# A half tile's inner rows are turned before the next unit's gate and up products, and its down product comes one unit after it instead of two

## The reference, cut to what matters

```python
logits = x @ gate_w.T                        # 64 experts, TOP_K = 8 of them per token
topv, topi = jax.lax.top_k(logits, TOP_K)
gu = jnp.einsum('nh,eih->nei', x, gu_w)      # gate and up rows, 2 x 128 inner
gate, up = (gu[..., :I], gu[..., I:])
inter = jax.nn.silu(gate) * up
inter_w = inter * W[:, :, None]              # routing weight, zero where not chosen
out = jnp.einsum('nei,ehi->nh', inter_w, dp_w)
```

## Time and profile before

| | |
|---|---|
| median of 3 runs | 970.89 us (968.95 to 973.75) |
| span of the profiled execution | 965.6 us |
| PE matmul busy | 872.5 us, 90% of the span |
| DVE, POOL, ACT busy | 465.5, 458.7, 214.3 us |
| mean of what DMA moved | 229 GB/s over the span |

### The profile page before, as it was taken

How to read it: one execution, slowest core, us unless ns; L and a number is a source line. 1 busy time by engine, 2 the same in 40 slices (tenths; PEclk the granted TensorE clock), 3 DMA queues, 4 the chain that set the end, 5 groups by cost and what they waited for, 6 DMA issues and landing times.

```text
span 965.6 us, 12358 instructions
## 1 busy us (share of the span) xinstructions
PE 872.5 (90%) x3437; PEld 514.2 (53%) x3437; DVE 465.5 (48%) x1177; ACT 214.3 (22%) x559; POOL 458.7 (48%) x447
## 2 busy tenths in 40 slices
PE   6999989989988694979989998999999999986997
PEld 2434534534534343657666665666666666763442
DVE  4797785788586540423323323333233333324496
ACT  2022221321312111212232222322223222321000
POOL 1420055236355766357556666566665656655000
PEclk9999999999998697989999999999999999998999
DMA  9951003103003152788898998889998997899997
GB/s 341 326 163 71 1 8 96 45 2 104 1 1 115 41 190 73 229 289 277 289 322 272 339 323 315 307 286 338 325 319 302 311 333 262 283 354 402 382 419 315
DMA packets 76927, 221.36 MB, mean 229 GB/s; under 512 B 19078, under 2 KB 19462, under 8 KB 76472
## 3 DMA queue, kind: packets, MB, share of 16 engines
q1 hardware_dynamic: 48760, 149.12, 43.9%
q0 software_dynamic: 28096, 71.42, 21.0%
HBM read 183.98 MB, written 48.87 MB: 241 GB/s over the span
## 4 chain that ended last, share of the span: by engine, by line
PE 60%; issue 8%; DVE 7%; another core or an unknown queue 7%; DMA 4%; SPq 3%; ACT 2%; ACTq 0%; POOL 0%; DVEq 0%; POOLq 0%
PE bank L2026 17%; PE bank L2046 8%; PE bank L1798 7%; PE bank L2016 5%; PE bank L1845 5%; PE bank L1911 3%; PE bank L2136 3%; DMA front<-y_rows 3%; PE bank L2037 2%; PE bank L1809 2%; SPq L668 2%; PE bank L2054 1%; PE bank L1930 1%; DMA front<-h_rows,gid_fixed 1%
## 5 line engine op out<-in xcount | busy, mean ns | idle before, releaser
L2026 PE MATMUL bank<-h2T,wqkv 128*128 128x256 f32 x1024 | 243.1, 388 | 9.9 <-issue 9.6
L719 POOL DMA_INDIRECT slot_table<-pair,place x128 | 130.4, 1019 | 183.3 <-DVE place L1262 118.2
L2026 PEld LDWEIGHTS bank<-h2T,wqkv 128*128 128x128 f32 x1024 | 193.1, 194 | 41.1 <-issue 16.5
L775 POOL DMA_INDIRECT y_rows<-front,tbl x110 | 113.6, 1033 | 83.8 <-DVE front L1641 38.1
L766 POOL DMA_INDIRECT front<-h_rows,gid_fixed x112 | 115.8, 1034 | 69.1 <-issue 31.6
L2046 PE MATMUL bank<-wqkv,front 128*128 128x512 f32 x256 | 127.9, 621 | 11.2 <-DVE front L1622 7.5
L1641 DVE TENSOR_SCALAR front<-bank,wgt 128x512 f32<-128x512 f32 x146 | 107.1, 748 | 43.3 <-DMA y_rows<-front,tbl 19.8
L1006 ACT ACTIVATE h2T<-bank 128x512 f32<-128x512 f32 x148 | 82.2, 595 | 161.4 <-issue 65.6
L1798 PE MATMUL bank<-wqkv,front 128*128 128x512 f32 x256 | 113.5, 594 | 0.0
L1622 DVE TENSOR_TENSOR front<-bank,front 128x256 f32<-128x256 f32 x64 | 27.2, 424 | 177.4 <-ACT front L1016 135.2
L2016 PEld LDWEIGHTS bank<-const,front 128*128 128x128 f32 x592 | 69.1, 143 | 62.0 <-issue 47.4
(11 more groups left out here) (292 smaller groups left out, 860.1 us busy)
## 6 DMA issues: line engine op xcount, KB each, us to landing
wqkv<-in_experts SPq DMA_DIRECT2D x64, 768.0 KB
front<-in_experts SPq DMA_DIRECT2D x36, 512.0 KB
front<-y_rows SPq DMA_DIRECT2D x20, 768.0 KB, 12.4
front<-in_experts SPq DMA_DIRECT2D x36, 256.0 KB
wqkv<-y_rows SPq DMA_DIRECT2D x12, 768.0 KB, 13.4
front<-in_w_mod SPq DMA_DIRECT2D x5, 1024.0 KB, 10.1
x<-in_x SPq DMA_DIRECT2D x4, 1024.0 KB, 10.8
h_rows<-h SPq DMA_DIRECT2D x4, 1024.0 KB
```

The costliest lines, as they stand in the source:

```text
L719: pool.indirect_dma_start(out=slots[:, :], out_offset=bass.IndirectOffsetOnAxis(ap=place[b % 2][:, i, k:k + 1], axis=0), in_=pair[:, b * T ...
L775: pool.indirect_dma_start(out=y_rows[:, :], out_offset=bass.IndirectOffsetOnAxis(ap=to, axis=0), in_=yb[s], in_offset=None, bounds_check=P ...
L2026: mm = pe.matmul(pair_bank[u % 2][:, j * PAIR:(j + 1) * PAIR], w[:, at:at + INNER], xT[u % 2][:, k, :], start=(k == 0), stop=(k == KC - 1))
```

## The change

On PE the turning of a half unit's inner rows moves from behind the gate and up products of the next unit to ahead of them, right behind the next tokens' transpositions. Its down product moves from two units behind to one unit behind, so that each unit now has exactly one unit's down products. DVE's scaling of the half tile and SP's wait for its down product move with it. After a half unit R the order on PE becomes: products of R, down of R-1, turn tokens of R+2, **turn inner rows of R**, products of R+1, **down of R**, turn tokens of R+3, products of R+2, down of R+1.

```diff
@@ -635,10 +635,8 @@
             for u in range(BODY_UNITS + 1):
                 if u in REST_UNIT:
                     next_rest_gu(u)
-                if u - 2 in REST_UNIT:
-                    after_down(UNIT[u - 2][0])
-                if u > 3 and u - 1 not in REST_UNIT:
-                    after_down(UNIT[u - 1][1])
+                if u > 3:
+                    after_down(UNIT[u - 1][-1])
@@ -1645,8 +1643,8 @@
             def taken(u, r):
-                for b in [u - 2] * (u - 2 in REST_UNIT) + [u - 1] * (u >= 1 and u - 1 not in REST_UNIT):
-                    for n in UNIT[b]:
+                if u:
+                    for n in UNIT[u - 1]:
                         take_y(n, r)
@@ -2084,15 +2082,16 @@
             def downs(u, r):
-                if u - 2 in REST_UNIT:
-                    n = REST_UNIT.index(u - 2)
-                    pe.wait_ge(s_rest_down, 32 * (n + 1))
-                    down_rest(u - 2)
-                if u >= 1 and u - 1 not in REST_UNIT:
+                if u - 1 in REST_UNIT:
+                    pe.wait_ge(s_rest_down, 32 * (REST_UNIT.index(u - 1) + 1))
+                    down_rest(u - 1)
+                elif u:
                     down(u - 1, r, slot_of(u - 1))
 
             def body(u):
                 turn(u + 1, 0)
+                if u - 1 in REST_UNIT:
+                    turn_inter(u - 1)
                 if u == 0:
                     pe.wait_ge(s_sht, TPB * (HELD + 1))
                 if u == 1:
@@ -2105,8 +2104,6 @@
                     gate_up(u, 0, slot_of(u))
-                if u - 1 in REST_UNIT:
-                    turn_inter(u - 1)
                 downs(u, 0)
```

## The result

| | before | after |
|---|---|---|
| median of the timed executions of this comparison | 968.83 us (964.38 to 975.74, 20 runs) | 977.53 us (969.81 to 984.79, 20 runs) |
| time and span of the profiled execution | span 965.6 us | 979.93 us, span 978.1 us |

The ratio is 1.0081, 95% interval 1.0057 to 1.0105: the change makes the kernel slower by 0.8%. Every timed execution of the changed kernel carries a span and a clock of its own (1.8 to 1.9 us between its time and its span, median clock 0.960 over the twenty), so the timed executions do what the profiled one does; that undoes the choice on which the forecast stood.

What follows compares the result with a forecast made beforehand. PE was taken as the bound, lacking 15.3 of 376 us. Minus 1.3 (bank wait), minus 0.9 (seams) and 0 for the rest gave a span of 963.4, with 5.3 us above the span 968.7 us; range 957 to 1003.

Steps and rivals of the forecast that it cites:

- The down product: Half tile's down product on PE, one unit earlier: bank wait gone, minus 1.3 us; cheaper seams between matmul groups, minus 0.9.
- the faster rival: Late marks are real, but the new order covers them where they cost PE: minus 13 us, 958 us; chance 0.17.
- The transposition: Turning of inner rows on PE: its new wait for silu and product, 0.65 us, has 2.70 us of cover, costs 0.
- The disputed term: Whether PE's marks, up to 5.9 us late to ACT in the profile, are late in timed executions; the forecast chose no.
- DVE: 0: DVE's copy of turned rows is never late and one scaling moves a unit earlier: 0 in either direction.
- SP and POOL: 0: SP's wait and loads and the half tile's scatter come earlier: taken as 0, ends minus 2 and plus 2 us.
- slower, by the new wait: PE stalls at the turning for late marks, 8 times 3.9 and 8 times 0.7 us: plus 20, 991 us; chance 0.28.
- Slower, with the clock: Each 3.9 us stall also halves PE's clock for 3.3 us, 13 us more: 1004 to 1018 us; chance 0.05.
- The sum and the range: Minus 2.2 us on the 965.6 us span, plus 5.3 us: 968.7 us, no change; range 957 to 1003 us.
- The marks come once PE stands still: PE's standstill at the turning releases late marks, stalls of 1.3 us in 8 to 16 units: 964 to 975 us; chance 0.10.

Runs made afterwards that it cites:

- e12: Changed kernel without POOL's gathers of the body's tiles from 16 on, scatters kept; one execution, span 935.8 us, 0.969 of the kernel before.
- e14: Changed kernel with the gathers of the body's tiles from 16 on cut to 16 of 128 rows; one execution, 1.004 of the kernel before.
- e2: Kernel before with only the half unit's down product moved to one unit behind, right behind the unmoved turning; 955.51 us against 958.69, ratio 0.9957.
- e1: Kernel before with only the turning of inner rows moved ahead of the next unit's products; 998.5 us against 958.69, ratio 1.0407.
- e13: Kernel of e10 with the half unit's down product moved behind the next tokens' transpositions; 963.88 us against 967.99 for the kernel before, ratio 0.9931.
- e10: Changed kernel with the turning of inner rows amid the next pair unit's up products; 952.9 us against 959.68 for the kernel before, ratio 0.9922.
- e3: Changed kernel with the turning of inner rows between the next unit's gate and up products; 949.72 us against 958.69 for the kernel before, ratio 0.9912.
- e4: Changed kernel with half units' gate and up products over the whole array, not two column halves; one execution, 1.008 of the kernel before.
- e7: Changed kernel with the gathers of the body's tiles from 16 on cut to 64 of 128 rows; one execution, 1.014 of the kernel before.
- e11: Changed kernel with a pause of POOL (two multiplications) for each half unit from tile 16 on; one execution, 970.07 us against 959.68, 1.011.

## Why the prediction was wrong, point by point

- *PE is the bound, DMA's share isn't waited for*: right, though the 15.3 us that PE was said to lack are 17.4 by the rows (L2016 has 1.5 us more, put down to "issue"). In e12 PE is busy for 310.00 of 310.00 us at a DMA share of 0.76, and e14 at 0.75 still loses 20 us of 340.
- *The down product: minus 1.3 us for the bank wait, minus 0.9 for the seams*: right in sign, small. 619 to 603 ns over 191 matmuls is 3.1 us. e2 shows what was left out: the half tile's down product ahead of the transpositions is cover for ACT's copy, and the 10.3 us of those waits go. This was the faster rival's mechanism, priced there at 7 us; it is real (0.5 us are left).
- *The transposition: "Then the new wait costs 0"*: this is the step that failed, by the choice made under *The disputed term*, that timed executions lack the lateness. They have it. In place of 0, PE's idle time at the turning is 28.3 us, and 0.8% of the time is lost. The timed ratios stand in the order of the profiles' idle time of PE: 36.8 us in e1 (1.0407), 29.6 in the changed kernel (1.0081), 17.4 before (1), 15.3 in e2 (0.9957), 11.9 in e13 (0.9931), 10.4 in e10 (0.9922), 7.4 in e3 (0.9912). In order, not in size: e1 loses twice what its idle time explains.
- *DVE: 0*: right in the changed kernel, whose half down products (L2052) wait 0.0 us. *SP and POOL: 0*: right for their own time, wrong as a ground for leaving them. POOL's order of instructions decides when a mark comes. The working looked for what PE and DMA did while the mark was out, and not for POOL, whose run of ten instructions in the kernel before ends at 523.85 (522.82 plus 1.03), 1.5 us before the silu of the earlier trace rows:

```profile
522.82 1.03 POOL L766 DMA_INDIRECT front<-h_rows,gid_fixed  x1 [0.31 <-issue]
```

- *The rival "slower, by the new wait"* (991 us) had the mechanism and its place. Its rule, that a mark costs what it is late beyond 2.1 us, fits nine of the ten: the half unit that is 5.0 us late makes PE wait 2.8 us, those that are 3.0, 5.6 and 7.6 us late 0.9, 3.4 and 5.5 us (in the tenth PE had waited elsewhere before). But it took all 16 late marks over, at 3.9 and 0.7 us. Measured are 28.3 us in ten waits, one of 5.5, seven of 2.6 to 3.5 and two of 0.9 us, and no wait in the other eight half units, whose marks are now at most 0.9 us late. The half that it priced at 0.7 us each cost nearly nothing, the rest 28 in place of 31.
- *"Slower, with the clock"* (0.05) came true in part: the granted clock fell to 0.50 behind five more stalls than before, at most 10 us by the gate and up matmuls where 13 were priced, and the stage's busy time rose by only 2.2 us. The two rivals belonged together, and the chance of both was too low.
- *The sum and the range*: the forecast set the time 5.3 us above the span, where the listed executions have 1.8; the ratio doesn't depend on it. That 977.5 us lies within 957 to 1003 is owed to the rivals for which the range was drawn wide, not to the mechanism that was chosen.
- *The marks come once PE stands still*: wrong. PE stood for 2.8 us in the stretch shown and the mark came with the end of POOL's run; in e2 and e10 marks come while PE is working.
- *The Trainium skill's rule* (Perfetto Trace Analysis, "Summary: the profiler window per engine type": a mark's way to the next engine is hidden in TensorE's rows): the trace agreed with it, and so do the timed runs now; its reading gave 991 us, on the right side. The Trainium skill, TensorE: Matmul & The Clock Gate, section "Why this matters for your kernels", puts each semaphore increment of a matmul at some 26 ns. No run here shows that figure for a mark alone; a silu that isn't held starts 0.04 us behind its products, and behind POOL's runs of eight and more most were 4.4 to 5.9 us late.

## What to carry to other kernels

A wait on a mark of TensorE needs cover for the lateness that the profile shows (the consumer's start less the producer's end), not for the producer's own time: if rows show 5 us, price the wait by them and don't put them down to the recording without a reason; here the timed executions had them. Each mark of a chain needs such cover of its own. When a mark is late, look at POOL too, and count its gathers and scatters in a row; and judge a cure by the sum of the lateness over all units, since a disturbance moves it from one to the next.

## What the runs showed of the hardware

- Marks of PE come out late while POOL issues indirect DMAs one behind the other (every 1.34 us), and nearly always 0.5 to 1.8 us after one of them ends (168 of the 180 marks over 2.5 us late in the profiles of all kernels but e4 and e12), four times in five the last of the run. Lateness goes with the run: in the changed kernel and e7 the marks that came behind runs of 8 were 4.4 to 5.3 us late, those behind runs of 10 5.4 to 5.6; one behind a run of 12 was 7.6; but one of 4.7 us came behind a run of 3, and the kernel before had 5.8 to 5.9 behind runs of 10 and also behind some of 6. One in five came out in the middle of a run, and many marks within runs were on time; what decides that, and by what path POOL holds PE's marks, is open. That it is the number of gathers and not their bytes rests on e12 against e14, one execution each, and on e12 before and after its gathers come back.
- Only PE's marks were late, to ACT and to DVE. Those of ACT and DVE were not where this was looked up: in all 18 half units of the changed kernel DVE's product starts 0.03 us behind ACT's silu, and a turning that waits starts 0.06 us behind that product.
- The clock falls behind some stalls and not others: in the changed kernel it fell to 0.50 at waits of 2.8, 2.8, 3.2, 3.4 and 5.5 us and once behind three short ones (0.5, 0.8 and 0.9 us, from 607.6 to 611.1 us), and not at waits of 2.6, 2.7 and 3.5 us; in e14, with seven waits up to 3.4 us, the stage's clock stayed 1.00. What tells them apart is open.
- e3 is the best version, 0.9% faster than the kernel before. That shorter runs of POOL would give much more is suggested by e12 (0.969 of the kernel before), but e12 leaves the gathers out, and no kernel with all its work and shorter runs was tried but e11, whose pauses only moved the late marks.
